# First expert stage of a two-layer perceiver: two accumulators, five weight buffers, key stacks loaded earlier

## The reference

```
shared = (silu(xf @ sg) * (xf @ su)) @ sd                # every token
top 4 of 8 groups, then top 4 of 32 experts, softmax gates; at most 80 tokens an expert
buf    = xf rows gathered per expert                     # 32 x 80 x 256
h      = silu(buf @ wg[e]) * (buf @ wu[e])               # 256 -> 512
out_e  = h @ wd[e]                                       # 512 -> 256
routed[token] += gate * out_e                            # scatter-add
x      = x + shared + routed
```

## Time and profile before

| | us |
|---|---|
| median of 3 runs | 1830.51 |
| their range | 1829.75 to 1830.67 |
| profiled execution | 1837.91 |
| its span | 1836.0 |

### The profile page before, as it was taken

The page is one execution under the profiler, slowest core; times in us unless marked ns, Lnnn a source line. Parts: engine busy times, 40 slices in busy tenths (PEclk is TensorE's granted clock), DMA queues, the critical chain, the costliest instruction groups (busy, mean ns, idle before and its releaser), DMA issues. The chain is left out here.

```text
span 1836.0 us, 36684 instructions
## 1 busy us (share of the span) xinstructions
PE 1669.6 (91%) x12555; PEld 1011.2 (55%) x12555; DVE 1135.5 (62%) x1992; ACT 859.6 (47%) x1768; POOL 227.3 (12%) x311
## 2 busy tenths in 40 slices
PE   7999969999999998868988998659999999989698
PEld 3444424444444445544858998525445445445598
DVE  6677758888888856436551111168888888836411
ACT  2222216777777765503521111127777777746132
POOL 1321220000000000000112433200000000000000
PEclk9999978999999999979998989869999999999699
DMA  6577765344444311000078989634434434221053
GB/s 188 183 207 202 201 158 75 59 69 63 57 69 63 58 49 56 1 1 0 2 186 256 291 270 288 219 56 70 67 55 69 66 54 69 35 45 51 0 184 104
DMA packets 144352, 192.52 MB, mean 105 GB/s; under 512 B 27351, under 2 KB 117976, under 8 KB 138044
## 3 DMA queue, kind: packets, MB, share of 16 engines
q1 hardware_dynamic: 137588, 187.24, 43.3%
q0 software_dynamic: 4608, 2.18, 0.7%
q10 hardware_dynamic: 2064, 1.87, 0.3%
HBM read 154.89 MB, written 39.44 MB: 106 GB/s over the span
## 5 line engine op out<-in xcount | busy, mean ns | idle before, releaser
L1188 DVE TENSOR_REDUCE top<-ps 128x1 f32<-128x1024 f32 x512 | 603.3, 1219 | 83.4 <-PE ps L1078 70.2
L1176 ACT ACTIVATE probs<-ps 128x512 f32<-128x512 f32 x1024 | 558.5, 600 | 203.4 <-PE ps L1099 191.0
L1099 PE MATMUL ps<-qst,kst 105*128 105x256 bf16 x2048 | 353.7, 275 | 7.4 <-DVE qst L1200 2.4
L1078 PE MATMUL ps<-kst,qst 105*128 105x512 bf16 x1024 | 316.5, 393 | 35.2 <-POOL qst L1032 28.9
L1099 PEld LDWEIGHTS ps<-qst,kst 105*128 105x128 bf16 x2048 | 169.8, 99 | 227.4 <-ACT probs L1176 85.7
L1113 PE MATMUL ps_o<-probs,vst 128*32 128x256 f32 x4096 | 274.1, 385 | 2.3 <-ACT probs L1176 2.3
L2072 PE MATMUL ps_h<-xe,wgu 128*128 128x80 f32 x1024 | 161.3, 280 | 12.9 <-ACT xe L2135 6.7
L1113 PEld LDWEIGHTS ps_o<-probs,vst 128*32 128x32 f32 x4096 | 106.8, 109 | 113.2 <-issue 51.3
L2072 PEld LDWEIGHTS ps_h<-xe,wgu 128*128 128x128 f32 x1024 | 147.6, 205 | 15.0 <-issue 7.4
L1078 PEld LDWEIGHTS ps<-kst,qst 105*128 105x128 bf16 x1024 | 90.1, 99 | 102.7 <-issue 60.3
L2242 DVE TENSOR_TENSOR hT<-silu,ps_h 128x320 f32<-128x320 f32 x32 | 15.6, 487 | 183.7 <-ACT silu L2142 157.0
(11 more groups left out here) (355 smaller groups left out, 1884.6 us busy)
## 6 DMA issues: line engine op xcount, KB each, us to landing
kst<-kd SPq DMA_DIRECT2D x384, 128.0 KB
kd<-kp SPq DMA_DIRECT2D x64, 384.0 KB, 2.8
wgu<-in_L_ffn_wg_dram SPq DMA_DIRECT2D x32, 512.0 KB
wgu<-in_L_ffn_wu_dram SPq DMA_DIRECT2D x32, 512.0 KB
wd<-in_L_ffn_wd_dram SPq DMA_DIRECT2D x32, 512.0 KB
w<-in_L_ffn_w_dram SPq DMA_DIRECT2D x16, 1024.0 KB, 5.6
ctx_sb<-in_ctx_dram SPq DMA_DIRECT2D x16, 512.0 KB, 5.7
vd<-square_weights SPq DMA_DIRECT2D x16, 512.0 KB, 4.2
```

The lines of the kernel that those rows point to most:

```text
L1078: mm = pe.matmul(ps1[:, slot1(m, u), x * 512:(x + 1) * 512], qst[:, m, qt * P:(qt + 1) * P], kst[:, m, c * W1 + x * 512:c * W1 + (x + 1) * ...
L1099: mm = pe.matmul(ps2[:, SCORES2[u], x, :], kst[:, m, kt * P:(kt + 1) * P], qst[:, m, :], start=True, stop=True)
L1176: nc.scalar.activation(probs[:, u % SLOTS, :, :], ps2[:, SCORES2[u], :, :], ACT.Exp).then_inc(probs_ready, 1)
L1188: v.tensor_reduce(top[:, b, u // NC1, u % NC1:u % NC1 + 1], ps1[:, slot1(m, u), :], AX, ALU.max).then_inc(mx, 1)
```

## The change

- `KeyStacks`, a new class, holds `kst` and its semaphores for the whole program. Layer 1's first four stacks are loaded (`begin`) by SP in layer 0's first `self_attention`.
- In `experts0` the weights have NW = 5 buffers, cut out of `vall`: 15 of its 16 parts make five slots, and expert e uses slot (e + 3) % 5. SP issues experts 0 to 2 at once, expert 3 when the first slots are ready, expert 4 when two experts are turned, then gate and up of e + 5 on `h_made` and down of e + 5 on `y_made` of expert e. The six weights of layer 1 are issued after expert 5's. All value parts are loaded at the end: parts 0 to 8 as experts 27, 28 and 29 are done, the other seven after the read-back.
- There are two accumulators in DRAM. The first begins as the residual, stored at the start; the second as the shared result (a copy of `acc`). Even experts scatter into the one, odd into the other, each waiting for the scatter two before. Result copies have YB = 4 buffers.
- Both accumulators are read back, and the norm is made in the same block, tile by tile, with 16 busy matmuls right after the last expert. `norm_phase` is no longer called there.
- `slots_of(0)` comes before `one_hot(1)`.

```diff
+class KeyStacks:
+    def __init__(self, pr, st):
+        self.kst = pr.sb(st, "kst", [XROWS, NBUF, SK], BF16)
+        self.k_in = [[pr.sem(st, f"k_stack_in{L}_{m}") for m in range(NBUF)] for L in range(2)]
...
+    def begin(self, eng, L):
+        for m in range(NBUF):
+            self.load_constant_rows(eng, L, m)
+            self.load_k(eng, L, m // B, m)
...
-        wgu, wd = sb("wgu", [P, 2, 2, C, F0]), sb("wd", [P, 2, FT0, D])
+        ring = next_cross.vall[:, 0:NW * PER * (B * KT // VPARTS), :].rearrange("p (w k) d -> p w (k d)", w=NW)
+        wgu = ring[:, :, 0:2 * C * F0].rearrange("p w (i c f) -> p w i c f", i=2, c=C)
+        wd = ring[:, :, 2 * C * F0:2 * C * F0 + FT0 * D].rearrange("p w (f d) -> p w f d", f=FT0)
...
-                for e in range(2):
+                sp.dma_start(yrows[0].rearrange("(t p) d -> p t d", p=P), residual[:, :, :]).then_inc(base_out[0], 16)
+                for e in range(NW - 1):
+                    if e == NW - 2:
+                        sp.wait_ge(slots_ready, 1)
                     load_gu(e)
                     load_d(e)
-                for m in range(NBUF):
-                    next_cross.load_constant_rows(sp, m)
-                    next_cross.load_k(sp, m // B, m)
-                for part in range(VSOON):
-                    next_cross.load_v(sp, part)
-                ahead(sp)
                 sp.wait_ge(base_ready, 1)
...
+                for e in range(E0):
+                    if e + NW < E0:
+                        sp.wait_ge(h_made, e + 1)
+                        load_gu(e + NW)
+                        sp.wait_ge(y_made, e + 1)
+                        load_d(e + NW)
+                    else:
+                        sp.wait_ge(y_made, e + 1)
+                        if e == E0 - 1:
+                            for i in range(2):
+                                sp.wait_ge(y_added[i], 16 * E0 // 2)
+                            for i, rows in enumerate((dst, y2)):
+                                sp.dma_start(rows[:, :, :], yrows[i].rearrange("(t p) d -> p t d", p=P)).then_inc(
+                                    y_back, 16)
+                        if slot(e) <= SLOT0 - 1:
+                            for part in range(PER * slot(e), PER * slot(e) + PER):
+                                next_cross.load_v(sp, part)
+                    if e == 0:
+                        ahead(sp)
+                for part in range(PER * SLOT0, VPARTS):
                     next_cross.load_v(sp, part)
...
-                    if e:
-                        pool.wait_ge(y_added, 16 * e)
+                    if e >= 2:
+                        pool.wait_ge(y_added[e % 2], 16 * (e // 2))
                     nc.gpsimd.indirect_dma_start(
-                        yrows, bass.IndirectOffsetOnAxis(token[:, e:e + 1], 0), ye[:, e % 2, :], None,
+                        yrows[e % 2], bass.IndirectOffsetOnAxis(token[:, e:e + 1], 0), ye[:, e % YB, :], None,
...
+                dve.wait_ge(y_back, 32)
+                moments(0)
+                for t in range(1, NT):
+                    moments(t)
+                    normalize(t - 1)
+                normalize(NT - 1)
...
-                           causal=False)
+                           causal=False, ahead=lambda sp: keys.begin(sp, 1))
...
-            norm_phase(pr, other, pr.xn, pr.xT)
```

More of the change, by code:

```diff
@@ L437, in _ @@
                         for m in range(NBUF):
-                            buffers.load_constant_rows(sp, m)
+                            buffers.keys.load_constant_rows(sp, 0, m)
                     if n in (6, 7):
@@ L446, in _ @@
                                 sp.wait_ge(k_out[q], 16 * NB // B)
-                        buffers.load_k(sp, (n - 10) // 2, n - 10)
+                        buffers.keys.load_k(sp, 0, (n - 10) // 2, n - 10)
                 for q in range(C):
@@ L450, in _ @@
                 for m in range(1, NBUF, B):
-                    buffers.load_k(sp, m // B, m)
+                    buffers.keys.load_k(sp, 0, m // B, m)
                 for q in range(C, NQ):
@@ L1019, in _ @@
                         wait_at(pr, sp, sc2, N2 * (g - NBUF + 1))
-                        buffers.load_k(sp, h, m)
+                        buffers.keys.load_k(sp, buffers.L, h, m)
                 if buffers.L == 0:
@@ L1844, in __init__ @@
         self.r_in, self.sh_in = pr.sem(st, "r_in"), pr.sem(st, "sh_in")
+        self.x_in = [pr.sem(st, f"x_in{i}") for i in range(4)]
+        self.y_added = [pr.sem(st, f"y_added{i}") for i in range(2)]
     def begin(self, sp, gate_rows, up_rows):
@@ L1947, in _ @@
[L1947 to L1958, removed]
@@ L1959, in _ @@
-                for part in range(VLATE, VPARTS):
-                    next_cross.load_v(sp, part)
-                sp.wait_ge(y_back, 16)
+                sp.wait_ge(base_ready, 1)
+                sp.dma_start(yrows[1].rearrange("(t p) d -> p t d", p=P), dst[:, :, :]).then_inc(base_out[1], 16)
+                sp.wait_ge(x_turned, 1)
+                load_gu(NW - 1)
+                load_d(NW - 1)
+                for e in range(E0):
[4 more added lines that the diff above has]
+                        load_d(e + NW)
+                    else:
+                        sp.wait_ge(y_made, e + 1)
[10 more added lines that the diff above has]
+                        ahead(sp)
@@ L1976, in _ @@
                     fetch(e)
-                pool.wait_ge(base_out, 16)
+                for i in range(2):
+                    pool.wait_ge(base_out[i], 16)
                 for e in range(E0):
@@ L2088, in down @@
                     mm = pe.matmul(ps_y[0:CAP0, b, half * P:(half + 1) * P], hT[:, b, f, :],
[L2089 removed]
+                                   wd[:, slot(e), f, half * P:(half + 1) * P], start=(f == 0), stop=(f == FT0 - 1))
                     if s == DOWN - 1:
@@ L2106, in _ @@
                             down(e, s - FIRST_DOWN)
+                for _ in range(BUSY_MATMULS):
+                    pe.matmul(ps_h[:, 0, 0, :], pr.cb("identb"), pr.constsb[:, 0:N], start=True, stop=True)
+                for t in range(NT):
+                    pe.wait_ge(normed, t + 1)
+                    for c in range(C):
+                        mm = pe.transpose(ps_h[:, t // 2, c, (t % 2) * P:(t % 2 + 1) * P], xn[:, t, c * P:(c + 1) * P],
+                                          pr.cf("ident"))
+                    mm.then_inc(n_turned, 1)
             @block.scalar
@@ L2152, in _, with root, copy_normed @@
                     act.wait_ge(y_made, e + 1)
-                    if e >= 2:
-                        act.wait_ge(y_added, 16 * (e - 1))
-                    nc.scalar.activation(ye[:, e % 2, :], ps_y[0:CAP0, e % 2, :], ACT.Copy,
+                    if e >= YB:
+                        act.wait_ge(y_added[e % 2], 16 * ((e - YB) // 2 + 1))
+                    nc.scalar.activation(ye[:, e % YB, :], ps_y[0:CAP0, e % 2, :], ACT.Copy,
                                          scale=share[:, e:e + 1]).then_inc(y_copied, 1)
+                def root(t):
+                    act.wait_ge(var_ready, t + 1)
+                    nc.scalar.activation(std[:, t:t + 1], std[:, t:t + 1], ACT.Sqrt).then_inc(std_ready, 1)
+                def copy_normed(pair):
+                    act.wait_ge(n_turned, 2 * pair + 2)
+                    nc.scalar.copy(xT[:, :, pair * 2 * P:(pair + 1) * 2 * P], ps_h[:, pair, :, 0:2 * P])
+                nc.scalar.activation(first_root[:, :], pr.cf("parity")[:, 0:1], ACT.Sqrt)
+                for t in range(NT - 1):
+                    root(t)
+                copy_normed(0)
+                root(NT - 1)
+                copy_normed(1)
             @block.vector
@@ L2601, in build @@
         moe0 = Experts0Start(pr, ctx)
+        keys = KeyStacks(pr, ctx)
         other = pr.sb(ctx, "other_x", [P, NT, D])
```

93 lines of the change are left out of this document (54 added, 39 removed).

## The result

| | before | after |
|---|---|---|
| median, us | 1830.59 (4 runs, 1829.75 to 1833.91) | 1808.08 (4 runs, 1806.65 to 1809.39) |
| profiled execution, its span | 1837.91, 1836.0 | 1809.39, 1807.5 |
| mean granted clock | 0.948 | 0.952 |

The ratio is 0.9874, 95% interval 0.9856 to 0.9891: 22.5 us faster. 1793.3 was forecast (37.2 won), with a range of 1785 to 1811. The sign was right. The time lies inside the stated range, but above the forecast's own 1788 to 1800; the forecast gain was two thirds larger than the measured one.

The account below looks back on a forecast made before the run. TensorE was taken as the bound, with late weight loads stalling the expert loop and late rows its front. Front 8.6, loop 28.6 and end 0 sum to 37.2 us off the 1830.5 median: 1793.3 us, range 1785 to 1811.

Parts of the forecast that it names:

- the end: From the last result copy to the query projection: 1.0 us won by the sum, taken as 0, bounds +1 and -4.
- rival 1: Expert loop: DMA is the bound, 27.7 us won, 1802.8 us; chance 0.14.
- rival 2: Expert loop: row fetches landing in 9 us become the wait, 15 us lost, 1808 us; chance 0.12.
- the front: Expert stage up to SiLU 1: it comes at 975.5 instead of 984.13 us, 8.6 us won.
- The pace: Loop from expert 1 to 31: five weight buffers remove all 28.6 us of stalls and their effects, leaving 158.7 us.
- the second accumulator: Scatters in the expert loop: none of POOL's waits is on TensorE's path now, so cost 0, with 2.6 us of cover.
- Key stacks: Loads moved from the stage's front to the first self-attention: 3.4 MB and 28 issues leave the front, cost 0.
- The first fetch: Stage's front: first row fetch lands in 5.1 us, bounds 5.1 and 10.5, so first products start 6.2 us earlier.
- The clock behind the first wait: Stage's front: TensorE idles some 2 us before the first products and the clock falls, charged at 3.3 us.
- The profile against the median: Whole kernel: profiled execution is 7.4 us above the median, unplaced; the whole gain is subtracted from the median, 1830.5 us.
- rival 3: Expert loop: row fetches at 10.5 us make loops of 6.9 us, 20 us lost, slower at 1844; chance 0.05.
- rival 4: Expert loop: the waits are the copy of xe, not weights; only the front pays, 1822 to 1824 us; chance 0.06.

Follow-up runs that it names:

- acc1: Changed kernel, but each scatter waits for the one just before it, as with one accumulator; five weight buffers stay: 1835.42 us.
- w2b: Changed kernel with two weight buffers and the kernel before's order of loads, remaining value parts every fourth expert and at the end; two scatter chains kept: 1827.95 us.
- keysback: Changed kernel with the key stacks loaded at the head of the expert stage again, behind the first three experts' weights: 1814.39 us.
- late: Changed kernel with the fourth and fifth experts' weights loaded only after the first rows are turned: 1801.63 us.
- warm: Changed kernel with ten dummy matmuls between the shared expert and the first turn: 1802.07 us.
- sems: Changed kernel with the expert stage's semaphores taken from the enclosing scope, given back only after the cross-attention: 1803.86 us.
- b_again: The kernel before, unchanged, run once more for a second profile: 1833.48 us in one run.
- w3: Changed kernel with three weight buffers, first loads issued at once, value parts beyond the ring one every fourth expert: 1801.90 us.

## Why the prediction was right, and where it was off

**The range.** The time lies 14.8 us above the forecast and outside the forecast's own 1788 to 1800. That own range left out the -4 that had been given to the end, and the end came to -3.35. The stated 1811 came from rivals 1 and 2, slower loops, and the loops were exactly as forecast: that the range held is luck in part. The 14.8 are made of the front (3.3), the end (3.35), the stage's start (2.1) and the profile's distance from the median (6.0).

**The pace.** The size was right, the reason only half. It read 28.6 us of stalls off the loop, and 28.6 went. It put them all on the weights and costed the second accumulator at 0, since in the rows of before TensorE is seen waiting for weights only. acc1 shows this to be wrong as a division: five buffers with one chain win nothing in the loop, and two chains with two buffers (w2b) nothing either. Both limits stand at 6.3 us an expert (SiLU 1 to 31 in 189.3 us in w2b and 189.95 in acc1), near the prediction's own arithmetic (3.4 of wait and 3 of work on POOL, "in step with the loop"). Whichever is lifted alone, the other holds. The gain belongs to the pair.

**Key stacks.** Right: no cost shows where they went, and keeping them at the stage's head costs 6.6 us in the front (keysback).

**The first fetch.** "5.1, the nearer in load" came to 6.2 until the turn. The 1.5 MB of the fourth expert, ordered 1 us ahead of the first fetch, made it so (late). The rows it was taken from are medians of several fetches, and only the first fetch counts here: it took 11.8 us before, where the median of the four was 10.5, and 6.2 after, where that median is 3.6; in the loop a fetch has such company too, but the 5.1 there are hidden. For the front 8.6 was forecast, and 5.3 won.

**The clock behind the first wait.** Charged at 3.3 us, read at 1063 in the loop. It cost 5.8 (warm): here the clock was 0.52 over 14.2 us, almost two experts. This is the term of the front that was mis-sized most.

**The end.** Taken as 0 within +1 and -4; it was -3.35. The read-back is issued 3.8 after the last result copy, not 3.0 (the last scatter starts 0.9 after the copy, behind an earlier one), the slowed projection costs 1.85, as forecast (about 2), and the block change takes 3.4 instead of 0.85; the read-back and the norm themselves took 0.9 less than the sum had. The block change was the unseen part: the 0.85 was that of the norm's own, small block, and sems shows that most of the 3.4 is the stage's semaphores.

**The start.** The stage began 2.1 later, which no term held; keysback shows the same without the loads, so chance is the likeliest reading. The terms of the profiles: 37.2 - 3.3 - 3.35 - 2.1 = 28.5.

**The profile against the median.** The other 6.0 us to 22.5 are the 7.3 by which the profile of before lay above its median, less 1.3 in the kernel after. The prediction took the whole sum off the median. In b_again's profile they don't lie in the loop's stalls. Which execution is the typical one stays open: in 37 runs on other chips the kernel before went from 1829.4 to 1847.6, with medians of 1833.3 to 1835.9, so the four runs that the 22.5 is counted from lie at the low end, and the gain may be larger elsewhere. The changed kernel wasn't run there.

**Rivals.** Rival 1 (DMA is the bound) did not come: the share is 0.95 in the loop, but SiLU 31 came 158.65 us after SiLU 1, on time. Rivals 2 and 3 needed fetches of 9 and 10.5 us in the loop; they land in 5.1 with the weight queue full. A rule of the Trainium skill ("DMA: Bandwidth & Descriptors", section "Queues, rings and completion order") was weighed there: that a write to a semaphore lands only after all earlier ones of its engine. The 5.1 beside loads that take 5.0 to 7.2 us to land (1050 to 1100 us) speak against a price of 10 us in the loop; whether the rule itself holds no run here shows. Rival 4 is refuted, since the loops are even at 5.16 and 5.81.

## What to carry to other kernels

When two resources have the same period, lifting one shows nothing: before costing an edit at zero, put the periods of all chains side by side, and price the pair. On TensorE a wait is priced with the clock behind it, and that price is read where the wait will be: two microseconds of idleness cost six more at the head of this loop. More buffers help only until the pace is met (here three, but for one load); beyond that, the early loads that fill them compete with the small transfer on which the start depends.

## What the runs showed of the hardware

- Row fetches with nearly idle queues are in SBUF at most 4.2 us after the first is issued (late, w3); beside 1.5 MB of weights it takes 6.0 to 7.2 (6.2 in after), with 3.4 MB of keys ahead of them as well 11.4 (keysback).
- Behind a wait of 1.8 us the clock was 0.52 over 14.2 us (after); in acc1 it was 0.75 over the 6.8 us behind a wait of 1.42, and stayed at 1.00 behind one of 0.73. Dummy matmuls over the same wait as in after kept it at 1.00 (warm).
- Giving back a stage's semaphores between two blocks took 2.75 us of TensorE's time (after and sems).
- An adding scatter of 80 rows took 6.4 us to land in the full loop (after).
